# Context attention: the maximum and the exponent offset of a unit move behind the next unit's first two score reads

## The chip, the cores and the metric

The kernel runs on one core of one Trainium2 chip. The metric is device time in microseconds: 2665.52 us is the median of three runs of the kernel before (2664.87 to 2669.96).

## The reference

Three layers act on x (4 x 128 rows of 1024): a cross attention to a context of 4 x 2048 rows, a causal self-attention, and a feed-forward layer with 4-bit weights. The change lies in the first:

```python
q = _fq_sym(q, axis=-1)          # 16 heads of 64, rounded to 8 bits
k = _fq_sym(k, axis=-1)
v = _fq_sym(v, axis=2)
attn = jnp.einsum('bhqd,bhkd->bhqk', q, k)
attn = jax.nn.softmax(attn.astype(jnp.float32), axis=-1)
attn = _fq_unsigned(attn, axis=-1)   # probabilities in 255 steps of their row's largest
out = jnp.einsum('bhqk,bhkd->bhqd', attn, v)
```

Every one of the 512 query rows sees all 8192 context rows, in each of 16 heads. The largest probability of a row is that of its largest score. So the kernel computes exp(scale * score - scale * max + ln 255), written as a 16-bit integer, and needs the row's maximum before the first exponential.

## The kernel before, in words

The stage is `attend_quantised`. A unit is one head and one tile of 128 query rows: 16 heads x 4 tiles are 64 units, taken as 8 pairs of heads, 8 slots to a pair (`n` from 0 to 7, `n // T` the head of the pair, `n % T` the tile). All buffers of a unit are doubled by `n % 2`.

A unit's 128 x 8192 scores come in eight chunks of 1024 columns. The positions 0 to 7 are the chunks `ORDER = (2, 3, 6, 7, 4, 0, 1, 5)`. For each chunk:

- TensorE (`scores`, L1388) makes two matmuls into one of two PSUM buffers, as soon as VectorE has read what was there two positions earlier.
- VectorE (`copy`, L1508) reads it into SBUF and takes its maximum per row in the same instruction. A read waits until the unit two earlier has done with that part of SBUF: for chunks 2 and 3 until its first exponential has run, for 6 and 7 until its second has, for 4 and 5 until TensorE has transposed its integers, for 0 and 1 until the DMA has. The last position is chunk 5. Its read waits for the fourth batch of transposes of the unit two earlier.

After the eighth read `find_max` (L1513) reduces the eight maxima to one, with a wait for the copies, and `make_bias` (L1520) multiplies it by the row's scale and adds ln 255, with a wait for `find_max`. ScalarE's first exponential of the unit (`exps`, L1598) waits for that offset.

ScalarE's queue has for slot n: first exponential of unit n (4096 columns), turned_out(n-1, 0) and (n-1, 1), second exponential of unit n, turned_out(n-1, 2) and (n-1, 3). `turned_out` (L1605) copies a batch of eight transposed blocks from PSUM to SBUF.

The integers of the first exponential are transposed by one DMA (`turn_probabilities`, L1286, issued by SyncE after waiting for the exponential, L1283), those of the second by TensorE in four batches k = 0 to 3 (`turns`, L1399), which share two PSUM buffers by `BANK = (0, 1, 0, 1)`. So batch 2 waits until ScalarE has copied batch 0 out, and batch 3 until batch 1 is out:

```python
pe.wait_ge(out_s, OUT0 + 4 * g + k - 1)
```

Everything is issued by a written order. In slot n and step c (0 to 7) TensorE does the scores two positions ahead (positions 2 to 7 of unit n+1, then 0 and 1 of unit n+2), and behind them in the same step (`finish_slot`), for unit n-1: transposes 0 and 1 in steps 0 and 1 (each followed by sums of unit n-2), the first half of the sums over the DMA's part (`dma_sums`, L1420, which waits for the DMA) in step 2, nothing in step 3, transposes 2 and 3 in steps 4 and 5, sums in steps 6 and 7. VectorE's `body` follows the same steps with its reads. In slots with n % T = 0 it also has `total_sum` (L1525, step 5) and `inverse` (L1529, step 6), in slots with n % T = 1 `output` (L1535, step 4, ahead of the last read's place in step 5).

On SyncE, VectorE, ScalarE and GpSimd the first and the last pair are written out, and the six pairs between are a loop whose waits compare with values computed in registers. TensorE's order is written out for all pairs. GpSimd rounds the next head's values (L1346 and on), which SyncE loads (L1205) behind the DMA transposes in its queue; the keys (L1200) come the same way.

Of the kernel before, what the change touches and what calls it, by code (L numbers as in the profile page):

```python
# [1208 lines left out]
def attend_quantised(chip, q_t, exp_scale, heads, v_scale, col, twice, o, ident32, ident16, x_d, x, stores, panels):  # L1209
# [8 lines left out]
    SLOTS = 2 * T  # L1218
# [26 lines left out]
    with ExitStack() as ctx:  # L1245
# [27 lines left out]
        def each_pair(eng, body):  # L1273
            body(0, True, False)
            with eng.Fori(1, PAIRS - 1) as i:
                body(i, False, False)
            body(PAIRS - 1, False, True)
# [212 lines left out]
        @block.vector  # L1490
        def _(dve):
            dve.sem_inc(copied, COPIED0)
            dve.sem_inc(inv_step, INV0)
            dve.sem_inc(o_taken, TAKEN0)

            def copy(i, n, pos):

                h, c = i * SLOTS + n, ORDER[pos]
                if c in (2, 3):
                    dve.wait_ge(exp_done, EXP0 + 2 * (h - 2) + 1)  # L1500
                elif c in (6, 7):
                    dve.wait_ge(exp_done, EXP0 + 2 * (h - 2) + 2)
                elif c in (4, 5):
                    dve.wait_ge(turned, TURNED0 + 4 * (h - 2) + 2 * (c - 4) + 2)
                else:
                    dve.wait_ge(dma_turned[n % 2], DMA0 + 16 * (i * (SLOTS // 2) + n // 2))
                dve.wait_ge(filled, h * CH + pos + 1)
                nc.vector.tensor_scalar(sc[n % 2][:, c * SC:(c + 1) * SC], score[pos % 2][:], 1.0, None, ALU.mult, ALU.max,  # L1508
                                        accum_out=part_max[n % 2][:, c:c + 1]).then_inc(copied, 1)

            def find_max(h, n):
                dve.wait_ge(copied, COPIED0 + (h + 1) * CH)
                nc.vector.tensor_reduce(neg_max[n % 2][:], part_max[n % 2][:], AX.X, ALU.max, negate=True)\  # L1513
                    .then_inc(bias_step, 1)

            def make_bias(h, n):

                dve.wait_ge(bias_step, h + 1)
                j, t = (n % SLOTS) // T, n % T
                nc.vector.tensor_scalar(bias[n % 2][:], neg_max[n % 2][:], qs_pair[j][:, t:t + 1], LN_TOP,  # L1520
                                        ALU.mult, ALU.add).then_inc(bias_ready, 1)

            def total_sum(head, j):
                dve.wait_ge(exp_done, EXP0 + 2 * T * (head + 1))
                nc.vector.tensor_reduce(total[j][:], part_sum[j][:], AX.X, ALU.add).then_inc(inv_step, 1)  # L1525

            def inverse(head, j):
                dve.wait_ge(inv_step, INV0 + 2 * head + 1)
                nc.vector.reciprocal(inv[j][:], total[j][:]).then_inc(inv_step, 1)  # L1529

            def output(head, j):
                dve.wait_ge(inv_step, INV0 + 2 * head + 2)
                dve.wait_ge(summed, SUMMED0 + 4 * T * (head + 1))
                dve.wait_ge(o_moved, MOVED0 + head + 1 - 2)
                nc.vector.tensor_tensor(o_pair[j][:], outp[j], inv[j][:].unsqueeze(2).to_broadcast((P, T, HD)),  # L1535
                                        ALU.mult).then_inc(o_taken, 1)

            def body(i, first, last):
                for n in range(SLOTS):
                    g = i * SLOTS + n  # L1540
                    for c in range(CH):
                        ahead, pos = (n + 1, c + AHEAD) if c + AHEAD < CH else (n + 2, c + AHEAD - CH)
                        if not (last and ahead >= SLOTS):
                            copy(i, ahead, pos)
                        done = None if n % T > 1 or first and n < 2 else 2 * i - 1 + n // T
                        j = (n // T + 1) % 2
                        if done is not None and n % T == 0 and c == 5:
                            total_sum(done, j)
                        if done is not None and n % T == 0 and c == 6:
                            inverse(done, j)  # L1550
                        if done is not None and n % T == 1 and c == 4:
                            output(done, j)
                        if c == 5 and not (last and ahead >= SLOTS):
                            find_max(i * SLOTS + ahead, ahead)
                            make_bias(i * SLOTS + ahead, ahead)

            for c in range(CH + AHEAD):
                copy(0, c // CH, c % CH)
                if c == 1:
                    dve.wait_ge(vs_turned, 1)  # L1560
                    nc.vector.tensor_reduce(col[:, 0, :], spread[1].rearrange("p (k n) -> p k n", n=P), AX.X, ALU.max)\
                        .then_inc(vs_step, 1)
                    dve.wait_ge(vs_step, 1)
                    nc.vector.tensor_scalar(col[:, 0, :], col[:, 0, :], 1.0 / LEVELS, 1e-8, ALU.mult, ALU.max)\
                        .then_inc(vs_step, 1)
                    dve.wait_ge(vs_step, 2)
                    nc.vector.reciprocal(col[:, 1, :], col[:, 0, :]).then_inc(vs_step, 1)
                    dve.wait_ge(vs_step, 3)
                    nc.vector.tensor_scalar(col[:, 0, :], col[:, 0, :], PROB_UNIT, None, ALU.mult).then_inc(vs_reduced, 1)
                if c == CH - 1:  # L1570
                    dve.wait_ge(q_ready, 2)
                    find_max(0, 0)
                    make_bias(0, 0)
            for stored, count in stores:
                dve.wait_ge(stored, count)
            each_pair(dve, body)
            total_sum(HEADS - 1, 1)
            inverse(HEADS - 1, 1)
            output(HEADS - 1, 1)
            dve.wait_ge(o_taken, TAKEN0 + HEADS)  # L1580
# [839 lines left out]
```

## Time and profile before

| | us |
|---|---|
| median of three runs | 2665.52 |
| the three runs | 2664.87, 2669.96, 2665.52 |
| profiled execution, span from first to last instruction | 2664.4 |
| mean granted TensorE clock | 0.977 of full |
| PE / VectorE / ScalarE / GpSimd busy over the span | 2483.9 / 2035.2 / 1093.7 / 873.8 |
| the 512 score reads (L1508) | 597.1 |
| the 128 exponentials (L1598) | 486.5 |

The profiled execution gives its span only: it ends within 1.2 us of the median, and within 0.5 us of the fastest run. The profile prints the span in 40 slices of 66.6 us. The stage of the change lies in slices 20 to 30, from the first score read at 1326.8 us to the last output at 1983.5 us. There VectorE and ScalarE are both at nine tenths or more in the middle slices, TensorE at eight. Around it, the projections before and the layers after are TensorE's. The stage ends before the next begins, so its length adds to the span as it is.

### The profile page before, as it was taken

The page shows a single profiled execution, that of the slowest core. Times are in us where ns is not written, and L with a number is a line of the kernel's source. Part 1 is how long each engine was busy: PE and PEld are TensorE (multiplying, and loading weights), DVE is VectorE, ACT ScalarE, POOL GpSimd, SP SyncE. Part 2 cuts the span into 40 slices and gives each one's busy share as a digit, 9 for nine tenths or more (in the row PEclk, how much of TensorE's full clock was granted, in tenths as well). Part 3 has the DMA queues.
Part 4 walks back from the last instruction along what each step waited for, and adds up shares of the span by engine and source line. Part 5 has one row for each costly group of instructions (what it writes and reads, how often), then busy time and mean ns, then how long its engine had stood idle before and what let it go on. Part 6 is the DMA issues. An engine that isn't in the chain of part 4 may idle for free. (4 is left out here: it accounts for less than half of the span.)

```text
span 2664.4 us, 42948 instructions
## 1 busy us (share of the span) xinstructions
PE 2483.9 (93%) x16296; PEld 1281.4 (48%) x16296; DVE 2035.2 (76%) x2932; ACT 1093.7 (41%) x1171; POOL 873.8 (33%) x432
## 2 busy tenths in 40 slices
PE   6999999999999999999978888888869999999998
PEld 3444444444444444444445555555544458444444
DVE  7898878778777877877699999999966344666664
ACT  4222222222222222222289999999982125211101
POOL 0233222322322232232166566566541651011100
PEclk9999999999999999999999999999999985999999
DMA  6234443443453344344479989989982331000000
GB/s 261 58 88 122 126 105 92 126 117 88 110 134 104 85 126 117 97 109 126 113 198 218 223 200 214 222 201 212 222 230 83 118 79 35 1 16 16 1 4 32
DMA packets 557347, 321.57 MB, mean 121 GB/s; under 512 B 401968, under 2 KB 533296, under 8 KB 552368
## 3 DMA queue, kind: packets, MB, share of 16 engines
q1 hardware_dynamic: 557232, 319.91, 47.0%
q8 instruction: 87, 1.43, 0.2%
q14 instruction: 28, 0.23, 0.0%
HBM read 149.95 MB, written 69.21 MB: 82 GB/s over the span
## 5 line engine op out<-in xcount | busy, mean ns | idle before, releaser
L1508 DVE TENSOR_SCALAR_CACHE_REDUCE at_sc<-at_score 128x1024 f32<-128x1024 f32 x512 | 597.1, 1220 | 12.5 <-PE at_score L1388 7.9
L1598 ACT ACTIVATE at_sc<-at_sc,at_bias,at_qs 128x4096 uint16<-128x4096 f32 x128 | 486.5, 3800 | 19.1 <-DVE at_bias L1520 18.4
L881 PE MATMUL kv_vacc<-wt_stage,kv_xthi 128*128 128x512 f16 x1024 | 388.1, 379 | 1.3 <-PEq L282 1.3
L881 PE MATMUL kv_vacc<-kv_wlo,kv_xthi 128*128 128x512 f16 x1024 | 388.1, 379 | 0.0
L881 PE MATMUL kv_vacc<-wt_stage,kv_xtlo 128*128 128x512 f16 x1024 | 388.1, 379 | 0.0
L889 PE MATMUL kv_kacc<-kv_wk,q_t 128*128 128x512 f16 x1536 | 347.2, 379 | 0.0
L960 ACT ACTIVATE q_t<-q_t 128x512 f16<-128x512 f32 x128 | 77.3, 628 | 488.9 <-POOL q_t L1163 327.8
L1161 POOL TENSOR_TENSOR q_t<-kv_rows 128x512 f32<-128x512 f32 x32 | 40.9, 1279 | 690.8 <-DMA kv_rows<-in_ctx 610.2
L889 PEld LDWEIGHTS kv_kacc<-kv_wk,q_t 128*128 128x128 f16 x1536 | 150.3, 98 | 181.2
L966 ACT ACTIVATE o<-wt_stage 128x1024 f16<-128x1024 f32 x64 | 67.7, 1058 | 407.0 <-DVE wt_stage L1052 407.0
L889 PE MATMUL kv_kacc<-kv_wk,kv_xthi 128*128 128x512 f16 x768 | 228.4, 379 | 0.7 <-DVE kv_xtlo L738 0.7
L1063 DVE SCALAR_TENSOR_TENSOR wt_stage<-kv_vacc,kv_bias 128x512 f32<-128x512 f32 x128 | 87.8, 686 | 175.9 <-PE kv_vacc L881 168.8
L1388 PE MATMUL at_score<-x,at_q 128*128 128x512 f16 x512 | 157.4, 390 | 61.2 <-DVE at_sc L1508 49.0
L1033 DVE SCALAR_TENSOR_TENSOR wt_stage<-kv_kacc,wt_stage 128x512 f32<-128x512 f32 x224 | 150.9, 686 | 80.6 <-PE kv_kacc L889 77.4
L1388 PE MATMUL at_score<-wt_stage,at_q 128*128 128x512 f16 x512 | 154.8, 384 | 53.6 <-DVE at_sc L1508 45.9
L1346 POOL TENSOR_TENSOR wt_stage<-wt_stage,at_vi 128x2048 f32<-128x2048 f32 x32 | 145.5, 4546 | 126.3 <-DMA wt_stage<-values 126.3
L1399 PEld LDWEIGHTS at_turn<-ident,at_sc 128*128 128x128 f16 x2048 | 136.4, 98 | 62.5 <-ACT at_sc L1598 2.9
L1028 DVE SCALAR_TENSOR_TENSOR q_t<-q_t 128x512 f16<-128x512 f32 x128 | 158.7, 1279 | 7.0 <-ACT q_t L960 7.0
L1174 POOL TENSOR_TENSOR wt_stage<-wt_stage,kv_bias 128x1024 f32<-128x1024 f32 x32 | 87.3, 2730 | 230.0 <-DVE wt_stage L1033 230.0
L1399 PE MATMUL at_turn<-ident,at_sc 128*128 128x128 f16 x2048 | 157.1, 220 | 3.2 <-ACT at_probt L1605 3.2
L881 PEld LDWEIGHTS kv_vacc<-wt_stage,kv_xthi 128*128 128x128 f16 x1024 | 100.2, 98 | 122.2 <-issue 1.7
L881 PEld LDWEIGHTS kv_vacc<-wt_stage,kv_xtlo 128*128 128x128 f16 x1024 | 100.2, 98 | 120.8
(246 smaller groups left out, 4242.6 us busy)
## 6 DMA issues: line engine op xcount, KB each, us to landing
kv_rows<-in_ctx SPq DMA_DIRECT2D x64, 512.0 KB, 7.0
values<-wt_stage SPq DMA_DIRECT2D x32, 1024.0 KB, 6.4
keys_turned<-o SPq DMA_DIRECT2D x32, 1024.0 KB, 5.1
wt_stage<-values SPq DMA_DIRECT2D x16, 2048.0 KB, 8.8
wt_stage<-keys_turned SPq DMA_DIRECT2D x32, 512.0 KB, 5.1
x<-keys_turned SPq DMA_DIRECT2D x31, 512.0 KB, 5.1
x<-in_x SPq DMA_DIRECT2D x2, 2048.0 KB, 8.6
kv_wk<-in_wq SPq DMA_DIRECT2D x2, 2048.0 KB, 12.7
```

The lines of the kernel that those rows point to most:

```text
L881: last = nc.tensor.matmul(v_acc[2 * s + c][:], a[s][:, k, :], b[:, c, k, :], start=(k == 0 and q == 0), stop=(k == KD - 1 and q == 2))
L889: last = nc.tensor.matmul(k_acc[bank][:], a[:, k, :], b[:, k, :], start=(k == 0 and q == 0), stop=(k == KH - 1 and q == 2))
L960: nc.scalar.activation(s_hi[:, n], s_rows[:, n], ACT.Copy, scale=X_SCALE).then_inc(s_hi_ready, 1)
L1028: nc.vector.scalar_tensor_tensor(out=s_lo[:, n], in0=s_rows[:, n], scalar=X_SCALE, in1=s_hi[:, n], op0=ALU.mult, op1=ALU.subtract).then_in ...
L1033: nc.vector.scalar_tensor_tensor(out=out, in0=k_acc[bank][:], scalar=UNSCALE, in1=other, op0=ALU.mult, op1=ALU.add).then_inc(k_taken, 1)
L1063: nc.vector.scalar_tensor_tensor(out=val[:, h:h + HALF // HD, s, :], in0=v_acc[2 * s + c][:].rearrange("p (h d) -> p h d", d=HD), scalar=U ...
L1174: nc.gpsimd.tensor_tensor(key[:, 0, :], key[:, 0, :], bias[:, 0:D], ALU.add)\
L1346: nc.gpsimd.tensor_tensor(v_raw[:, tiles], v_raw[:, tiles], vi_head[:].unsqueeze(1).to_broadcast((P, KVT // 2, HD)), ALU.mult).then_inc(v_ ...
L1388: last = nc.tensor.matmul(score[pos % 2][:, b * HALF:(b + 1) * HALF], q_pair[j][:, t * P:(t + 1) * P], kt[j][:, cols], start=True, stop=True)
L1399: last = nc.tensor.transpose(turn[BANK[k]][:, b, :], prob[n % 2][1][:, at:at + P].bitcast(F16), ident16[:])
L1508: nc.vector.tensor_scalar(sc[n % 2][:, c * SC:(c + 1) * SC], score[pos % 2][:], 1.0, None, ALU.mult, ALU.max, accum_out=part_max[n % 2][:, ...
L1598: nc.scalar.activation(prob[n % 2][e], sc[n % 2][:, e * EC:(e + 1) * EC], ACT.Exp, bias=bias[n % 2][:], scale=qs_pair[j][:, t:t + 1], accu ...
```

## The change

`find_max` and `make_bias` of unit n+1 stood together after the eighth read, in step 5. Now `find_max` stands in step 6, behind the read of position 0 of unit n+2, and `make_bias` in step 7, behind the read of position 1. Nothing is added or removed, and the other engines' orders are as they were. The offset of unit 0, made before the first pair, stays. In the last pair, where unit n+2 does not exist, the two instructions stand in the same steps without the reads.

```diff
                         if done is not None and n % T == 1 and c == 4:
                             output(done, j)
-                        if c == 5 and not (last and ahead >= SLOTS):
-                            find_max(i * SLOTS + ahead, ahead)
-                            make_bias(i * SLOTS + ahead, ahead)
+                        if c == 6 and not (last and n + 1 >= SLOTS):
+                            find_max(i * SLOTS + n + 1, n + 1)
+                        if c == 7 and not (last and n + 1 >= SLOTS):
+                            make_bias(i * SLOTS + n + 1, n + 1)
```

## Rows read from the trace of the kernel before

**Rows 1.** Waits of the six looped pairs: us in total, times, longest us.

```profile
PEld at_score L1388 <- DVE at_sc L1508: 136.1, 277, 1.0
ACT at_sc L1598 <- DVE at_bias L1520: 15.7, 48, 0.5
```

**Rows 2.** Lines L1520 and L1605, the same stretch: count, duration ns or busy us, mean ns.

```profile
L1520 DVE TENSOR_SCALAR at_bias<-at_nmax,at_qs x48: 212/214/216, 1431.5 to 1899.1; 128x1 f32<-128x1 f32 x48
...
L1605 ACT ACTIVATE at_probt<-at_turn 128x512 int32<-128x512 int32 x192 | 102.6, 586 | 0.0
```

**Rows 3.** Timeline of VectorE, two units: start us, us, engine, line, operation.

```profile
1499.73 1.23 DVE L1508 TENSOR_SCALAR_CACHE_REDUCE at_sc<-at_score 128x1024 f32<-128x1024 f32 x1
...
1509.64 1.23 DVE L1508 TENSOR_SCALAR_CACHE_REDUCE at_sc<-at_score 128x1024 f32<-128x1024 f32 x1
...
1510.79 0.16 DVE L1525 TENSOR_REDUCE at_total<-at_psum 128x4 f32<-128x8 f32 x1
1510.90 0.16 DVE L1513 TENSOR_REDUCE at_nmax<-at_pmax 128x1 f32<-128x8 f32 x1
1511.10 0.21 DVE L1520 TENSOR_SCALAR at_bias<-at_nmax,at_qs 128x1 f32<-128x1 f32 x1
1511.32 1.23 DVE L1508 TENSOR_SCALAR_CACHE_REDUCE at_sc<-at_score 128x1024 f32<-128x1024 f32 x1
...
1512.47 0.17 DVE L1529 RECIPROCAL at_inv<-at_total 128x4 f32<-128x4 f32 x1
1512.56 1.19 DVE L1508 TENSOR_SCALAR_CACHE_REDUCE at_sc<-at_score 128x1024 f32<-128x1024 f32 x1
...
1514.83 1.22 DVE L1508 TENSOR_SCALAR_CACHE_REDUCE at_sc<-at_score 128x1024 f32<-128x1024 f32 x1
1515.97 1.22 DVE L1508 TENSOR_SCALAR_CACHE_REDUCE at_sc<-at_score 128x1024 f32<-128x1024 f32 x1
...
1519.74 1.22 DVE L1508 TENSOR_SCALAR_CACHE_REDUCE at_sc<-at_score 128x1024 f32<-128x1024 f32 x1
```

**Rows 4.** Timeline of ScalarE, TensorE and SyncE in the first of these units.

```profile
1501.56 3.81 ACT L1598 ACTIVATE at_sc<-at_sc,at_bias,at_qs 128x4096 uint16<-128x4096 f32 x1 [0.39 <-DVE at_bias L1520]
...
1505.23 0.72 PEld L1420 LDWEIGHTS at_outp<-q_twice,at_probt_dma 128*128 128x128 f16 x16
...
1505.36 1.06 ACT L1605 ACTIVATE at_probt<-at_turn 128x512 int32<-128x512 int32 x2
...
1505.70 4.87 SPq L1286 DMA_TRANSPOSE at_probt_dma<-at_sc  x1
...
1507.52 0.65 PEld L1399 LDWEIGHTS at_turn<-ident,at_sc 128*128 128x128 f16 x8
1508.44 0.60 PE L1388 MATMUL at_score<-x,at_q 128*128 128x512 f16 x2
1508.88 0.61 PE L1399 MATMUL at_turn<-ident,at_sc 128*128 128x128 f16 x8
...
1511.35 3.80 ACT L1598 ACTIVATE at_sc<-at_sc,at_bias,at_qs 128x4096 uint16<-128x4096 f32 x1 [0.17 <-DVE at_bias L1520]
```

**Rows 5.** Line L1286, DMA issue to landing: all 64, then that of 1406.7 and of 1923.2.

```profile
DMA to landing us min/median/max: 6.6/7.2/9.4
...
DMA to landing us min/median/max: 9.3/9.3/9.3
...
DMA to landing us min/median/max: 8.8/8.8/8.8
```

**Rows 6.** Timeline of the stage's last units, where TensorE had to wait.

```profile
1966.73 1.07 ACT L1605 ACTIVATE at_probt<-at_turn 128x512 int32<-128x512 int32 x2
...
1967.46 0.61 PE L1399 MATMUL at_turn<-ident,at_sc 128*128 128x128 f16 x8 [0.41 <-ACT at_probt L1605]
...
1971.71 0.64 PE L1420 MATMUL at_outp<-q_twice,at_probt_dma 128*128 128x64 f16 x16 [2.73 <-DMA at_probt_dma<-at_sc]
```

**Rows 7.** A stretch after a long TensorE wait: engines' busy us, granted clock, DMA.

```profile
1361.00:1367.00 6.00, 5.60 (x62) 4.25 (x63) 2.62 (x5) 1.89 (x3) 1.29 (x5) 0.57 0.31 59
```

## The prediction

> **What bounds the kernel now.** I read four views. The waits of the six looped pairs come first [rows 1]. TensorE's longest total, 136.1 us, is for score reads on VectorE. ScalarE waits only for the offset, 48 times and 15.7 us in all, 0.33 us a unit, and VectorE waits for next to nothing. So VectorE paces, with ScalarE a third of a microsecond a unit behind. Line L1520 gives the pace [rows 2]: 48 offsets from 1431.5 to 1899.1 us, so 467.6 / 47 = 9.95 us a unit.
>
> The timeline of VectorE shows how a unit is made up [rows 3]. I call the start of a unit's last read (position 7) R. From R to the next R: 1499.73 to 1509.64, 9.91 us. Reads follow one another every 1.145 us (1514.83 to 1515.97). At the end of a unit stands a hole: the read lets the next operation start at 1510.79 and the next read starts at 1511.32, 0.53 us later, with the maximum and the offset between. Eight reads and this hole make 1.15 + 7 x 1.145 + 0.53 = 9.70. The other 0.2 us stand ahead of R, which waits for transposes 3: TensorE begins them at 1508.88 behind scores 7 at 1508.44 [rows 4], and scores 7 follow the end of the read of position 5 by 0.14.
> A group of four units has a slot with the total and the reciprocal (0.09 more, 1512.47 to 1512.56) and the output ahead of R: 1509.64 to 1519.74 is 10.10. So four units take 3 x 9.90 + 10.10 = 39.80 us, which is 9.95 each and agrees with [rows 2]. In the written-out pairs a wait costs VectorE some 0.1 us less behind a hole and the pace is about 9.69.
>
> **The change on VectorE.** Both instructions lose their wait, because a read of 1.145 us stands between. What a small operation costs without a wait is shown: the reciprocal delays the next read by 0.09, though it lasts 0.17 [rows 3]. By the same overlap of 0.08, the maximum (0.16) costs 0.08 and the offset (0.21) 0.13. Bounds: 0 each, if wholly covered, and what they take now, 0.53 together. I take 0.21. VectorE alone would save about 0.3 us a unit.
> The Trainium skill ("VectorE: DVE Perf Modes", section "The DRAIN you can't avoid") says that the next operation doesn't start before the pipe is empty and that the semaphore costs nothing extra. By it the hole would shrink by nothing. The trace does not bear it out here: the total starts at 1510.79, 0.08 before the read at 1509.64 with its 1.23 is over, the maximum 0.11 later, and the reciprocal in the same way. By the rule the loop below would be 0.2 longer, which is the dearer-operations rival.
>
> **What it does to ScalarE.** This decides the sum. The offset's instruction now starts when the read of position 1 is over. From R: 1.15 (read), 1.145 (position 0) + 0.08 (maximum), 1.145 (position 1) = 3.52. The exponential starts 0.25 after the offset's start (1511.10 to 1511.35): R + 3.77. Before it was R + 1.71 (1509.64 to 1511.35). It is 2.06 us later against the reads, and everything ScalarE and SyncE hang on it.
>
> Follow unit U. After its first exponential ScalarE takes turned_out(U-1, 0), which frees the PSUM buffer of transposes 2. TensorE holds that batch in its queue ahead of scores 7 and transposes 3, and the next R waits for those. Now: exponential at 1501.56, copy-out 0 at 1505.36 (3.80 later), done 0.59 later [rows 2] at 1505.95, and transposes 2 start loading at 1507.52 [rows 4]. That is a slack of 1.46 us after a latency of 0.11 (1966.73 + 0.59 = 1967.32 to a load at 1967.43 and a matmul at 1967.46 [rows 6]). A delay of 2.06 us is more than the slack, so a closed loop forms: R, two reads, offset, exponential, copy-out, transposes 2, scores 7, transposes 3, R. Its length:
>
> 3.77 (to the exponential) + 3.80 + 0.59 (copy-out) + 0.14 (to the matmul) + 0.44 (transposes 2, the issue pitch of scores 7 to transposes 3 at 1508.44 and 1508.88) + 0.44 (scores 7) + 0.76 (transposes 3 at 1508.88 to R at 1509.64) = 9.94 us.
>
> VectorE alone would need 1.15 + 1.225 + 1.275 + 4 x 1.145 + 0.14 + 0.44 + 0.76 = 9.57. ScalarE's own queue needs 9.62: it goes idle 0.17 ahead of 1511.35, having begun at 1501.56 [rows 4]. Both are below 9.94, so the loop sets the pace. VectorE's freed 0.3 us turns up as a longer hole ahead of R.
> To four units are added what now lies on the loop: total and reciprocal, 0.17, and 0.11 for the exponential of a head's first tile, which waits for one more semaphore (in [rows 3] and [rows 4], R 1499.73 to exponential 1501.56 is 1.83 against 1.71). The output (0.33) hides in the hole. So 4 x 9.945 + 0.28 = 40.06 against 39.80: +0.26 for four.
> - Looped pairs, 48 units: +3.2 us.
> - Written-out pairs, 11 paced units: the loop is 0.11 shorter there, 9.83 against 9.69, +0.14 each; in the two groups' output slots it is even. Together +1.4 us.
> - Start: TensorE's stop until 1361.4 for the values of the first heads covers the shift. 0.
> - End: after the last R the stage is ScalarE's chain, which starts from the exponential of unit 62, two reads later: +2.0 us.
>
> **What it does to the DMA transposes.** Their issue follows the exponential by 4.14 (1501.56 to 1505.70), so R + 7.91. TensorE wants the result in step 2 behind the next R. Its load comes at R + 5.50 now (1505.23 [rows 4]) and would at R + 5.2 with the first hole gone, so a landing of more than 9.94 + 5.2 - 7.91 = 7.2 us makes TensorE wait. The median of all 64 is 7.2, the longest 9.4 [rows 5]. About half will wait, where one, by 0.2 us, did in the middle of the stage. Not each wait costs time, since TensorE runs a read ahead and R has its hole. A landing after L delays R, by way of the load and the sums' issue (0.55, an estimate from their 0.63 in [rows 6]), scores 5 (0.60 [rows 4] and 0.1 to the read), the read (1.145), scores 7 (0.14 + 0.44) and transposes 3 (0.76): R comes at landing + 3.74 at the earliest, that is 11.65 + L after the R two before, against 19.88. So L over 8.2 costs. In the 64 landings, looked at one by one, seven are well over: 9.3 (1406.7, first [rows 5]), 9.2, 8.7, 9.3, 9.2, 9.3, and 8.8 (1923.2, last [rows 5]). They recur every 80 us, in the slot whose transposes go beside the load of the next values. Their excess over the limit is 1.2 + 1.0 + 0.5 + 1.1 + 1.0 + 1.1 + 0.7 = 6.6 us; those of 8.2 to 8.5 fall mostly in slots with extra length. I take 6.4. Bounds: 0, if the landings keep to their median, and 12, if each over 7.7 costs its excess. GpSimd gets its values 2 us later; its rounding has 5 us and more to spare before the sums need them, so 0.
>
> **Sum.** 3.2 + 1.4 + 0 + 2.0 + 6.4 = +13 us on the profiled span of 2664.4, so 2677.4, and on the median of 2665.5, 1.1 us above it: 2678.5.
>
> **The rivals.**
> - *VectorE's gain arrives.* If transposes 2 were not held up, the pace would be max(9.57, 9.61) plus the extras: some 0.29 less a unit over 59 units, 17 us, less 2.0 at the end: 2650.5. For it: ScalarE has only 0.33 us of waiting a unit and its queue fits into 9.61. Against: it decides at a slack of 2.06 us ahead of transposes 2, and the rows show 1.46, plus at most the 0.3 by which the reads run faster, which works the wrong way. 7%.
> - *The loop alone, DMA hidden.* 3.2 + 1.4 + 2.0 = +6.6: 2672. For it: the hole ahead of R and TensorE's lead of one read. Against: landings of 9.2 and 9.3 are over the limit by 1 us. 15%.
> - *Even.* The loop is 0.1 us shorter than my sum of nine terms (-6) and the DMA costs less: within 5 us of now. 11%.
> - *Dearer small operations.* The maximum and the offset keep their present cost and lie twice in the loop: +0.2 a unit, 12 us more: 2690. 6%.
> - *TensorE's clock falls.* After a 3.9 us stop the stretch 1361 to 1367 ran at a granted 0.57, 1.2 GHz for most of it [rows 7]. The new waits of up to 2.2 us at seven places would each be followed by scores, transposes and sums at half rate, 0.44 more for each batch of them on the loop, three batches and 1 to 2 us each: 2689. Against: after a wait of 2.73 us the sums at 1971.71 ran at the full 2.4 GHz rate [rows 6]. 6%. The Trainium skill ("TensorE: Matmul & The Clock Gate", section "HAM oscillation — how this bites in real kernels") has a kernel in which each wait for a DMA sent the clock back; by that rule this rival would be the forecast.
>
> **How the numbers follow.** The forecast holds 55%: 2678.5, with 0.1 us a unit of doubt on the loop (6 us) and the DMA's 0 to 12. The range 2668 to 2689 takes in the loop alone and most of the dearer cases; it leaves out the gain. One can't tell less than 0.2%, 5.3 us, from no change. Faster: 7%. Same: the even case and a part of the second, 14%. Slower: 79%.
>
> **What would show it.** In the trace after: the maximum starts right at the end of a read, without its 0.12, and the exponential 3.8 after R instead of 1.7; ScalarE's wait for the offset goes from 0.33 to some 0.4 us a unit; transposes 2 wait for a copy-out (L1399 for L1605, absent now from the middle) by some 0.6 us a unit; the hole ahead of R grows to about 0.5; waits of L1420 for the DMA appear in about half of the units; the offsets come every 10.0 to 10.15 us. I am wrong if the offsets come every 9.7 us or less, or if transposes 2 do not wait.

## The result, and the profile after

The changed kernel takes 2685.59 us (median of 4 runs, 2684.38 to 2689.29) against 2666.34 us before; the ratio on record, an estimate and not the quotient of the two medians, is 1.0069 with the 95% interval [1.0055, 1.0084]. It is slower by some 19 us, where 13 were forecast: 2678.5, with a range of 2668 to 2689 that holds the result. The span of the profiled execution grew from 2664.4 to 2683.7 us, by 19.3.

The waits of the looped pairs come first, as in [rows 1] (columns: total us, times, longest). PEld is TensorE's loading of weights, PE its matmuls.

```profile
PEld at_score L1388 <- DVE at_sc L1508: 87.4, 181, 1.0
...
PEld at_turn L1399 <- ACT at_probt L1606: 36.3, 42, 1.0
PEld at_outp L1420 <- DMA at_probt_dma<-at_sc: 28.3, 20, 3.2
ACT at_sc L1599 <- DVE at_bias L1520: 23.4, 49, 2.4
```

Two rows are new: transposes wait for a copy-out of ScalarE, and sums wait for the DMA, 20 times in some 48 units. TensorE waits less for VectorE's reads, and ScalarE's wait for the offset grew from 15.7 to 23.4 us. Line L1520 gives the pace, which was 9.95 us [rows 2]:

```profile
L1520 DVE TENSOR_SCALAR at_bias<-at_nmax,at_qs x48: 206/210/211, 1430.3 to 1905.1; 128x1 f32<-128x1 f32 x48
```

474.8 / 47 = 10.10 us a unit. The timeline shows one unit, from its last read (R, 1526.96) to the next R (1536.83), in VectorE's, ScalarE's, TensorE's and SyncE's rows:

```profile
1526.96 1.23 DVE L1508 TENSOR_SCALAR_CACHE_REDUCE at_sc<-at_score 128x1024 f32<-128x1024 f32 x1
...
1528.11 1.22 DVE L1508 TENSOR_SCALAR_CACHE_REDUCE at_sc<-at_score 128x1024 f32<-128x1024 f32 x1
...
1529.25 0.16 DVE L1513 TENSOR_REDUCE at_nmax<-at_pmax 128x1 f32<-128x8 f32 x1
1529.33 1.22 DVE L1508 TENSOR_SCALAR_CACHE_REDUCE at_sc<-at_score 128x1024 f32<-128x1024 f32 x1
...
1530.46 0.21 DVE L1520 TENSOR_SCALAR at_bias<-at_nmax,at_qs 128x1 f32<-128x1 f32 x1
...
1530.59 1.21 DVE L1508 TENSOR_SCALAR_CACHE_REDUCE at_sc<-at_score 128x1024 f32<-128x1024 f32 x1
...
1530.71 3.80 ACT L1599 ACTIVATE at_sc<-at_sc,at_bias,at_qs 128x4096 uint16<-128x4096 f32 x1 [0.21 <-DVE at_bias L1520]
...
1534.51 1.06 ACT L1606 ACTIVATE at_probt<-at_turn 128x512 int32<-128x512 int32 x2
1534.84 14.71 SPq L1286 DMA_TRANSPOSE at_probt_dma<-at_sc  x2
1535.13 0.45 PEld L1399 LDWEIGHTS at_turn<-ident,at_sc 128*128 128x128 f16 x8 [0.87 <-ACT at_probt L1606]
...
1535.63 0.60 PE L1388 MATMUL at_score<-x,at_q 128*128 128x512 f16 x2
...
1536.07 0.61 PE L1399 MATMUL at_turn<-ident,at_sc 128*128 128x128 f16 x8
...
1536.83 1.23 DVE L1508 TENSOR_SCALAR_CACHE_REDUCE at_sc<-at_score 128x1024 f32<-128x1024 f32 x1
```

The read after R starts at once, the maximum costs 0.08 and the offset 0.13. The exponential starts at R + 3.75, where it was R + 1.71 [rows 3, 4]. Its copy-out now holds up transposes 2, for 0.87 us by the row at 1535.13, and R stands 0.76 behind transposes 3. The loop is closed, at 9.87 us here.

The second wait shows in the very next unit. The DMA transpose issued at 1534.84 lands 9.1 us later, and this is what hangs on it:

```profile
1543.95 0.52 PEld L1420 LDWEIGHTS at_outp<-q_twice,at_probt_dma 128*128 128x128 f16 x16 [2.08 <-DMA at_probt_dma<-at_sc]
...
1545.07 1.23 DVE L1508 TENSOR_SCALAR_CACHE_REDUCE at_sc<-at_score 128x1024 f32<-128x1024 f32 x1 [1.09 <-PE at_score L1388]
...
1547.56 1.23 DVE L1508 TENSOR_SCALAR_CACHE_REDUCE at_sc<-at_score 128x1024 f32<-128x1024 f32 x1
```

The next R comes at 1547.56, 10.73 us after 1536.83, where undisturbed ones at this place in the group of four come 9.83 apart.

A third thing was not forecast: a stop at 1402 to 1407 us, in the first pair. The timeline of VectorE, SyncE and TensorE there:

```profile
1359.72 0.16 DVE L1513 TENSOR_REDUCE at_nmax<-at_pmax 128x1 f32<-128x8 f32 x1
1364.10 1.23 DVE L1508 TENSOR_SCALAR_CACHE_REDUCE at_sc<-at_score 128x1024 f32<-128x1024 f32 x1 [4.22 <-PE at_score L1388]
1365.24 0.21 DVE L1520 TENSOR_SCALAR at_bias<-at_nmax,at_qs 128x1 f32<-128x1 f32 x1
...
1369.54 4.87 SPq L1286 DMA_TRANSPOSE at_probt_dma<-at_sc  x1
1374.45 0.58 SPq L1205 DMA_DIRECT2D wt_stage<-values  x1
...
1407.60 0.77 PE L1408 MATMUL at_outp<-q_twice,at_probt 128*128 128x64 f16 x16 [5.02 <-POOL q_twice L1352]
```

Unit 2's maximum was ready at 1359.9. Its offset stands behind the read of position 1, and that read waited 4.22 us for scores behind TensorE's first stop. So offset, exponential and DMA transpose came late, and with them the load of head 1's values, which stands behind this transpose in SyncE's queue: 1374.45, where it was 1369.07 before. TensorE then waited 5.02 us for GpSimd to round these values, and behind this wait, from 1407.6 to 1411, its granted clock was 0.55.

The 19.3 us, from the R of each unit in both traces:

| stretch | before | after | difference |
|---|---|---|---|
| start to R of unit 1 | 1347.0 | 1347.6 | +0.6 |
| R of unit 1 to R of unit 8 | 73.3 | 79.2 | +5.9 |
| R of unit 8 to R of unit 55 | 467.5 | 474.8 | +7.3 |
| R of unit 55 to R of unit 63 | 78.4 | 80.3 | +1.8 |
| R of unit 63 to the end | 698.2 | 701.9 | +3.6 |

Each stretch is one profiled execution against one. The ten profiled executions of the experiments below have the R of unit 1 at 1347.6 to 1349.4 us, whatever they change, so the +0.6 ahead of unit 1 is not shown to be an effect of the change.

### The profile page after: what moved, and what is told of

Same layout as the page of the kernel before. It is cut to its first block and busy times, and to the rows that moved or that the text cites. A ratio compares the mean times of both kernels' runs of the same rounds, so it can differ in the third digit from the quotient of the medians.

```text
span 2683.7 us, 42948 instructions
## 1 busy us (share of the span) xinstructions
PE 2488.7 (93%) x16296; PEld 1275.1 (48%) x16296; DVE 2024.5 (75%) x2932; ACT 1092.9 (41%) x1171; POOL 874.5 (33%) x432
## 5 line engine op out<-in xcount | busy, mean ns | idle before, releaser
L1399 PEld LDWEIGHTS at_turn<-ident,at_sc 128*128 128x128 f16 x2048 | 130.5, 99 | 113.5 <-ACT at_probt L1606 44.7
```

The source lines that it names most:

```text
L1399: last = nc.tensor.transpose(turn[BANK[k]][:, b, :], prob[n % 2][1][:, at:at + P].bitcast(F16), ident16[:])
```

## The experiments

The theory: the late exponential costs by three ways, the loop through ScalarE's copy-out, DMA transposes that land too late for the sums, and head 1's values. The rivals: VectorE itself pays for the new places, or the loop alone sets the time.

**Both behind the read of position 0.** The exponential is then only one read late.

```diff
-                        if c == 7 and not (last and n + 1 >= SLOTS):
+                        if c == 6 and not (last and n + 1 >= SLOTS):
                             make_bias(i * SLOTS + n + 1, n + 1)
```

> Maximum and offset of unit n+1 both behind the read of position 0 (step 6), none behind position 1. Theory (the loss comes from the offset being 2.06 us later than the slack of 1.46 us ahead of transposes 2, and from what hangs on the exponential): the exponential starts about R + 2.75, 1.0 us later than before the change, so transposes 2 never wait, hardly any sums wait for the DMA, the values of head 1 are in time, and VectorE keeps most of its gain: the pace is ScalarE's 9.6 to 9.7 us, the time 2646 to 2657 us, below the kernel before. Rival (the instructions' new places cost VectorE itself, whatever ScalarE does): about half way between the two kernels or above, 2673 to 2686 us.

Measured: 2662.16 us, ratio to before 0.9983 [0.9973, 0.9993]. Direction and mechanism are the theory's: the exponential at R + 2.73, and no row for transposes that wait for a copy-out. But the size was missed. The undisturbed pace is 9.67 us in three units of four and 9.95 in the one with the output, and waits for the DMA remain:

```profile
PEld at_outp L1420 <- DMA at_probt_dma<-at_sc: 12.2, 13, 2.4
```

In the looped pairs they cost 3.8 us over the undisturbed pace. The pairs still take 461.4 us, 6.1 less than before; the end of the stage, which hangs on the later exponential of unit 62, takes 1.6 more. VectorE keeps a hole of 0.32 us, since the offset still waits for the maximum right ahead of it. The time is below the kernel before, so the rival of VectorE's places falls.

**Maximum at once, offset behind the read of position 0.**

```diff
+                        if c == 5 and not (last and n + 1 >= SLOTS):
+                            find_max(i * SLOTS + n + 1, n + 1)
                         if c == 6 and not (last and n + 1 >= SLOTS):
-                            find_max(i * SLOTS + n + 1, n + 1)
-                        if c == 7 and not (last and n + 1 >= SLOTS):
                             make_bias(i * SLOTS + n + 1, n + 1)
```

> Maximum at once behind the eighth read as before the change, offset behind the read of position 0. Theory: the exponential starts at about R + 2.65; same pace as with both behind that read, 2646 to 2657 us, the hole behind the eighth read 0.2 us and none between maximum and offset. Rival (the place in VectorE's queue costs): 2673 to 2686 us.

Measured: 2667.54 us, 1.0000 [0.9991, 1.0010], between the two expectations. The pace is 9.82 us in three units of four, so this order of the two instructions costs 0.15 us a unit more there than the one above. R of unit 6 to 7 took 13.94 us, in the version above 11.51. This is not a longer wait for head 1's values: TensorE's matmuls waited 3.02 and 2.95 us for them. What differs is the granted clock behind the wait, 0.51 (all but the lower of its two levels, 1.2 GHz) against 1.00 (2.4 GHz). These rows are of this version and of the one above. They give the stretch, its length, the busy us of PE, PEld, VectorE, ScalarE and GpSimd (with the number of instructions), the granted clock, and the DMA's share and GB/s:

```profile
1404.00:1411.00 7.00, 5.79 (x59) 4.15 (x60) 2.96 (x7) 4.80 (x4) 2.77 (x6) 0.51 0.96 300
...
1404.00:1411.00 7.00, 5.73 (x92) 3.98 (x93) 5.16 (x9) 6.98 (x5) 2.23 (x6) 1.00 0.88 295
```

In the same 7 us TensorE made 59 matmuls here, 92 there.

**Unit 2's offset in its old place**, the rest as changed.

```diff
-                        if c == 6 and not (last and n + 1 >= SLOTS):
+                        old = first and n == 1
+                        if c == (5 if old else 6) and not (last and n + 1 >= SLOTS):
                             find_max(i * SLOTS + n + 1, n + 1)
-                        if c == 7 and not (last and n + 1 >= SLOTS):
+                        if c == (5 if old else 7) and not (last and n + 1 >= SLOTS):
                             make_bias(i * SLOTS + n + 1, n + 1)
```

> The changed kernel, but unit 2's maximum and offset in their old place. Theory (TensorE's 5 us stop near 1402 us comes from the values of head 1, which are loaded behind unit 2's DMA transpose, and that waits for unit 2's exponential, held back 6 us by a read that TensorE's first stop delays): the stop goes, 5 us less than the changed kernel, 2680.5 us (2679 to 2682). Rival (the stop is set by GpSimd's own pace and is only shown elsewhere): no change, 2685.5 us.

Measured: 2682.45 us, 1.0059 [1.0042, 1.0075]. In the trace the stop is gone: R of unit 1 to R of unit 8 takes 73.6 us instead of 79.2. One unit's offset made this stop. Of the 5.6 us the medians show 3.1; in the profiled run the looped pairs and the stretch behind them were each 1.7 us longer than in the changed kernel. Late landings are one part of it, TensorE's clock the other. It fell three times here, behind matmuls' waits of 1.94 to 2.29 us for a DMA transpose (at 1619.5, 1824.2 and 1906.1). The first of them:

```profile
1620.00:1624.00 4.00, 4.00 (x28) 2.46 (x25) 2.38 (x4) 4.00 (x3) 3.92 (x2) 0.57 0.84 159
```

Behind two landings of the same 9.6 us the time from R to R was 12.30 us where the clock fell and 11.29 where it did not, so this fall cost about 1 us. The two intervals overlap, so the gain in time is not shown beyond noise, the stop's cause is.

**The values' loads cut to an eighth**, the rounding fed from the scales. This version leaves out seven eighths of the values of every head but the first, so its output is not the reference's.

```diff
+        part = slice(0, KVT if isinstance(head, int) and head == 0 else KVT // 8)
-        sp.dma_start(self.v_raw, self.v_d[bass.ds(head, 1)].rearrange("a p n d -> (a p) n d"))\
+        sp.dma_start(self.v_raw[:, part], self.v_d[bass.ds(head, 1), :, part].rearrange("a p n d -> (a p) n d"))\
...
-                    nc.gpsimd.tensor_tensor(v_raw[:, tiles], v_raw[:, tiles], rounder, ALU.add).then_inc(v_step, 1)
+                    nc.gpsimd.tensor_tensor(v_raw[:, tiles], vi_head[:].unsqueeze(1).to_broadcast((P, KVT // 2, HD)), rounder, ALU.add).then_inc(v_step, 1)
```

> The changed kernel with the loads of the values cut to an eighth for all heads but the first, and the rounding fed from the scales instead; the output for these is not the reference's. Theory (the long landings of the DMA transposes come beside the values' load, and cost about 12 us by delaying the last read of every fourth unit): landings fall to 6.7 to 7.5 us, waits of the sums for the DMA go, 12 us less, and up to 5 us less for the early stop: 2668 to 2674 us. Rival (the loop through ScalarE alone sets the time, landings are hidden): 2681 to 2686 us.

Measured: 2667.09 us, 0.9999 [0.9990, 1.0009], 18.5 us below the changed kernel and 1 to 2 us below the range expected. Transposes wait for copy-outs no less than in the changed kernel, but the pace is below that of the kernel before:

```profile
L1521 DVE TENSOR_SCALAR at_bias<-at_nmax,at_qs x48: 206/208/212, 1424.7 to 1890.4; 128x1 f32<-128x1 f32 x48
...
PEld at_turn L1400 <- ACT at_probt L1607: 42.6, 48, 1.0
...
PEld at_outp L1421 <- DMA at_probt_dma<-at_sc: 12.7, 11, 1.4
```

465.7 / 47 = 9.91 us. Against the kernel before the loop alone costs nothing; the rival falls. In the looped pairs no landing took over 8.4 us, where seven of the changed kernel's 48 took 9.1 to 10.2 and four of the kernel before's took 9.2 to 9.3. The expectation had landings of 7.5 at most and no waits of the sums; landings of 8.1 to 8.4 and 12.7 us of waits remain, at next to no cost in time.

**Copy-out 0 ahead of the first exponential.** It opens the loop at its other end.

```diff
-                    exps(i, g, n, 0)
                     if not (first and n == 0):
-                        for k in range(2):
-                            turned_out(g - 1, k)
+                        turned_out(g - 1, 0)
+                    exps(i, g, n, 0)
+                    if not (first and n == 0):
+                        turned_out(g - 1, 1)
```

> The changed kernel, with copy-out 0 of the unit before put ahead of the first exponential in ScalarE's queue instead of behind it. Theory (transposes 2 wait for a copy-out that stands behind the late exponential): their waits for a copy-out, 0.87 us a unit now, go; the undisturbed pace falls from 9.83 to about 9.7 us, but the exponential starts 0.5 us later still and so do the DMA transposes, so that late landings cost some 6 us more: 2680 to 2688 us, about even. Rival (the loop through the copy-out is what makes the changed kernel slower): at least 10 us less than the changed kernel, below 2676 us.

Measured: 2690.16 us, 1.0089 [1.0073, 1.0106], 2 us above the theory's range. The least R to R is 9.53 to 9.82 us in three units of four, as low as VectorE allows, and yet the kernel is slower than the changed one: at every fourth unit R to R is 10.0 to 12.9 us, six times in eleven over 10.9, by the DMA. The three longest, 12.9, 12.7 and 12.5 us, each have a fall of TensorE's granted clock at the wait's end (near 1468, 1670 and 1834 us). The DMA's row:

```profile
PEld at_outp L1420 <- DMA at_probt_dma<-at_sc: 29.8, 28, 3.0
```

**A stand-in at the old place**, as an edit of the kernel before.

```diff
                         if c == 5 and not (last and ahead >= SLOTS):
                             find_max(i * SLOTS + ahead, ahead)
-                            make_bias(i * SLOTS + ahead, ahead)
+                            dve.wait_ge(bias_step, i * SLOTS + ahead + 1)
+                            nc.vector.tensor_scalar(stand_in[:], neg_max[ahead % 2][:], qs_pair[(ahead % SLOTS) // T][:, ahead % T:ahead % T + 1], LN_TOP,
+                                                    ALU.mult, ALU.add)
+                        if c == 7 and not (last and n + 1 >= SLOTS):
+                            make_bias(i * SLOTS + n + 1, n + 1)
```

> The kernel before's work at the old place kept (the maximum, and a stand-in for the offset that writes to a tile nobody reads), and the real offset in the new place, behind the read of position 1. It adds 64 small instructions. Theory (reads, maximum and offset lie on the loop): the exponential starts at R + 4.2, the undisturbed pace is 9.83 + 0.45 = 10.3 us, late landings cost less for it (8 us instead of 13), together 2703 to 2712 us. Rival (VectorE has slack in the changed kernel and lateness alone counts): 2686 to 2692 us.

Measured: 2698.00 us, 1.0124 [1.0107, 1.0141], below the theory's range and above the rival's. The exponential starts at R + 4.22 and the undisturbed pace is 10.3 us, as expected: what VectorE does between R and the offset lies on the loop with its full length. The miss is in the DMA's part. With units 0.45 us longer, late landings cost about 1.7 us in the looped pairs, summed over what a unit takes beyond the usual one at its place, not 8.

**The values' load in two halves**, on the changed kernel and on the version with both behind position 0. Each half has its own semaphore, the second is issued one slot later, and GpSimd waits for each half ahead of its rounding.

```diff
...
-                        heads.values(sp, 2 * i + 1)
+                        heads.half_values(sp, 2 * i + 1, 0)
+                    if n == (3 if first else 2):
+                        heads.half_values(sp, 2 * i + 1, 1)
...
-                        heads.values(sp, 2 * i + 2)
+                        heads.half_values(sp, 2 * i + 2, 0)
+                    if n == T + 2 and not last:
+                        heads.half_values(sp, 2 * i + 2, 1)
...
```

> The changed kernel with only the values' load cut in two in this way. Theory: of the 13 us that late landings cost, 6 to 10 go, and the early stop shrinks by up to 3 us since GpSimd starts on the first half sooner: 2672 to 2680 us. Rival (full DMA engines, order of no use): 2683 to 2688 us.

Measured: 2669.04 us, 1.0009 [0.9999, 1.0019]. 16.5 us less than the changed kernel, more than expected, with every byte still loaded. Landings in the looped pairs end at 8.3 us, and the pace is that of the cut loads:

```profile
L1531 DVE TENSOR_SCALAR at_bias<-at_nmax,at_qs x48: 206/210/213, 1425.8 to 1891.4; 128x1 f32<-128x1 f32 x48
```

That is 9.91 us. So 2 MB at once beside a transpose made the landings long. Not all of the gain is theirs: of the 17.2 us by which the two profiled spans differ, 9.3 are in the looped pairs, 1.8 in the pair behind them and 5.3 in the first pair, where GpSimd starts on the first half sooner: the matmuls' first stop is under 1 us instead of 4.3, and the second 2.6 us instead of 5.0.

> Maximum and offset both behind the read of position 0, and the load of a head's values cut into two halves, the second one slot later in SyncE's queue. Theory (the DMA transposes beside a values' load land late, 9.2 us instead of 6.7, because 2 MB come at once): the long landings fall to about 8 us, and with them the last 4 to 5 us of late reads: 2656 to 2660 us. Rival (the landings are long because the DMA engines are full over the whole head, and the half moved lengthens the next one): 2661 to 2666 us.

Measured: 2658.31 us, 0.9969 [0.9958, 0.9981]. The waits for the DMA shrink from 12.2 to 3.7 us and their cost to nearly nothing:

```profile
ACT at_sc L1610 <- DVE at_bias L1531: 4.1, 23, 0.2
PEld at_outp L1431 <- DMA at_probt_dma<-at_sc: 3.7, 11, 0.5
```

**Whose gain is it?** The kernel before with the split alone, and the last version again beside it.

> The kernel before (maximum and offset together behind the eighth read) with the values' load cut in two. Theory (before the change the DMA transposes' landings of up to 9.4 us were hidden, since their issue came 2 us earlier against the reads, so there was nothing for the split to win there): the pace stays 9.95 us, the time within 2 us of the kernel before, 2665 to 2669 us. Rival (the split is a gain of its own of some 4 to 16 us, whatever the place of the offset, and the last kernel's lead over the kernel before is the split's): 2650 to 2663 us.

> Maximum and offset behind the read of position 0 and the values' load cut in two, a second time beside the kernel before with the split, to set the two apart. Theory: 2657 to 2660 us, 7 to 9 us below both. Rival (the lead is the split's alone): the same time as the kernel before with the split.

Measured: 2668.41 us, 1.0003 [0.9994, 1.0012], and 2659.07 us, 0.9970 [0.9959, 0.9981]. The split brings nothing to the kernel before, where the landings were hidden. With the maximum and the offset behind position 0 it makes the fastest version, 8 us below the kernel before and 9 below that kernel with the split.

## Why the prediction was right, and where its sizes were off

The direction held, and the loop and the late landings are both in the trace where the forecast has them. The size was 13 us against 19. By its own terms, with the version with short loads as the measure of the loop:

| term | forecast | measured |
|---|---|---|
| loop, looped pairs | +3.2 | -1.7 (465.8 against 467.5) |
| loop, written-out pairs | +1.4 | +0.3 |
| start | 0 | +5.8 |
| late landings | +6.4 | +10.7 |
| end | +2.0 | +3.6 |
| ahead of unit 1 | none | +0.6 |

That the result lies in the range is in part luck. The loop was put 6.0 us too high, the other terms together 12.3 us too low, and the two errors partly cancel. More than a third of the 13 us forecast, 4.6, was to come from a longer loop, which gave 1.4 us back instead; what made the kernel slower are the landings, a stop in the first pair that the forecast put at nothing, and the end.

- *VectorE's small operations.* 0.08 and 0.13 forecast, 0.08 and 0.12 to 0.13 measured. Right, and the dearer-operations rival is out. The prediction set this against the Trainium skill ("VectorE: DVE Perf Modes", section "The DRAIN you can't avoid"), but left out a sentence of the same section, that an operation that is not held (made to wait for all in front of it) starts earlier. The early starts here agree with that sentence.
- *The exponential.* R + 3.77 forecast, 3.75 measured.
- *The loop.* It closed where it was said to, with 0.87 us of waiting ahead of transposes 2 in the unit shown and 36.3 us in the looped pairs, 0.76 a unit (0.6 forecast). Its length was put at 9.94 and is 9.83 to 9.87. The main term that was too long is from the copy-out to the matmul: 0.73 forecast, 0.63 measured (copy-out at 1534.51, load at 1535.13). With 40.06 us for four units it looked like a small loss; with 39.55 against 39.80 it is a small gain. So the loop is where VectorE's gain of 0.3 us a unit went (the version with both behind position 0, where it does not close, takes 9.74 a unit undisturbed against 9.89), but it cost nothing beyond.
- *Late landings.* The limit was right: the landing of 9.1 us put R 3.6 us behind it (3.74 forecast) and 0.9 late. The count was wrong. Sums waited 20 times, a little less than the half of the units that was forecast, but the landings beyond the limit were more and longer. The forecast took the landings as they were before. After the change, unit 30's, 38's and 46's transposes take 9.5, 10.2 and 9.3 us instead of 8.0, 7.6 and 7.6. In the looped pairs alone there are seven over 9 us, not four. 10.7 is the stretch from unit 8 to 63 against the run with short loads (9.0 + 1.7); against the run with the load in halves it is 11.1.
- *The start.* This step failed. "TensorE's stop until 1361.4 for the values of the first heads covers the shift" is true of the reads. But the shift of unit 2's offset is not two reads; it is two reads and the stop between them, 6.4 us, and head 1's values hang on it by SyncE's queue. And the rounding's margin of "5 us and more" before the sums holds for later pairs only: in the kernel before it ends at 1400.8 in the first pair and the sums start at 1401.1, a margin of 0.4 us; in the next pair 1472.9 and 1480.2. So even one read's delay makes a stop, 2.95 us in the version with both behind position 0.
- *The end.* From the last R to the stage's last instruction it took 22.2 us, 18.6 before. Of the 3.6 us, 2.0 stand ahead of the DMA's last landing, and they are the forecast term: the last exponential ends 12.09 us behind the last R, 10.27 before, and four versions with the offset in the new place (unit 2's in the old, short loads, the stand-in, the load in halves) have an end of 20.1 to 20.4 us. The other 1.6 us are TensorE's clock in this execution. From the last landing to the output, 80 matmuls took 4.8 us at a granted 0.61, and 3.1 us at 0.97 before (after, then before):

```profile
1998.10:2002.90 4.80, 4.64 (x80) 4.52 (x80) 0.02 (x1) 1.19 (x2) 0.00 (x0) 0.61 0.93 386
...
1980.40:1983.50 3.10, 2.99 (x80) 2.87 (x80) 0.00 (x0) 1.09 (x2) 0.00 (x0) 0.97 0.95 396
```

  The kernel before with the split, its offset in the old place, shows an end of 21.7 us, with a landing of 10.1 us and a clock fall as well.
- *TensorE's clock.* In the looped pairs of the profiled execution it stayed at 1.00, after matmuls' waits of up to 2.7 us too, so that rival is out there; in the first pair and at the end it fell. Its mechanism is real all the same: with unit 2's offset in its old place and with copy-out 0 ahead, it fell at the end of DMA waits of 1.94 to 2.46 us, six times in all, and cost about 1 us in the one case where two equal landings can be compared. Other executions of the changed kernel may have such falls; none but one is profiled. The kernel in the section of the Trainium skill that the prediction cites ("TensorE: Matmul & The Clock Gate", "HAM oscillation — how this bites in real kernels") waited 3 to 5 us for each DMA, so it is no forecast for waits of 2.2 us; neither every wait here nor none brought the clock down.

## What to carry to other kernels

An instruction moved later on the pacing engine gains its hole and delays all that waits for its result. Before it is moved, the slack of each of these consumers is to be read, behind the first one too: here a copy-out two steps on had 1.46 us, a DMA result landing after the median 7.2 us had 2.4 (issue at R + 5.85, load at R + 5.50 one unit later), one landing after 9.3 only 0.3, and the delay was 2.06. One read later instead of two stays within the first, and the DMA's slack can be made by cutting a large load that runs beside it: no landing in the changed kernel's looped pairs was then over 8.3 us. Where the schedule has an irregular start, the delay is counted there by itself: an instruction behind work that stalls takes over the whole stall.

## What the runs showed of the hardware that was not expected

- A DMA transpose of a 128 x 4096 tile took 6.6 to 6.7 us at the least. When the load of 2 MB came in the slot before, it took 7.8 to 10.2 us in the changed kernel's looped pairs, over 9 in seven cases of twelve. With the load in two halves of 1 MB a slot apart, at the same total, no transpose of these pairs took over 8.3 us (8.5 in the other versions with the split).
- How long these transposes take depends on where they fall: the same loads and the same order with a shift of 2 us made three of them 1.5 to 2.6 us longer (units 30, 38 and 46), and the version with unit 2's offset in its old place repeats it (9.8, 9.6 and 9.6 us, against 8.0, 7.6 and 7.6 in the kernel before). Single landings also differ by up to 1.8 us between two executions of one kernel.
- A matmul's wait of 1.94 us for a DMA was followed by a granted clock of 0.57, and one of 2.7 us by a clock that stayed at 1.00, in two versions whose looped pairs have the same order. Which waits bring it down is not settled by these runs.
- Two small operations behind the read of position 0, with the offset's wait between them, lengthen its pitch from 1.145 to 1.46 us (1521.37 to 1522.83). The maximum at once behind the eighth read lengthens that pitch to 1.48 (1533.84 to 1535.32), and the offset one read later costs 0.12 more. A wait for the read that has just ended costs more than the wait between the two operations.
